# A gated cross-attention block on one core: weight work on other engines, and projections two slots later

## The chip, the cores and the metric

The kernel runs on 1 core of a Trainium2 chip, as one launch. Its engines are TensorE (PE in the profile; PEld is its weight loading), VectorE (DVE), ScalarE (ACT), GpSimd (POOL) and SyncE (SP), which here issues every DMA. The metric is the device time in microseconds; less is better. Each engine works through its own program in order, and the programs meet only at semaphores.

## The reference

One Flamingo-style block on x (4 batches of 512 rows by 512) with a context of the same size, cut to what matters here:

```python
ln  = layernorm(layernorm(x))                              # the second with weights and bias
fp8 = lambda x, s: e4m3(bf16(clip(x / s, -448, 448)))      # back in f32
q, k, v, qx = (fp8(ln, s) * s @ W.T * w_scale for s, W, w_scale in ...)   # 16, 8, 8, 16 heads of 128
kx, vx = split(ctx @ w_kv_x.T)
q, k, qx, kx = head-wise layernorms
core = softmax(q k^T / sqrt(128)) v                        # two query heads share a key head
xout = softmax(qx kx^T / sqrt(128)) vx
x = x + tanh(g0) * (fp8(concat(core, xout), smooth) * ... @ wproj.T)
# feed-forward part, weights in {-1, 0, 1} times a scale
ternary = lambda w: clip(round(w / mean|w|), -1, 1) * mean|w|
h = int8(layernorm(x)) @ ternary(w_gate_up).T;  a, b = split(h)
x = x + tanh(g1) * (int8(silu(a) * b) @ ternary(w_down).T)
```

Products that need f32 accuracy are made of pairs of f16: x = hi + lo, with `hi = f16(x)` and `lo = f16(x - hi)`.

## The kernel before, in words

The attention part is cut into 32 rounds (`it`): 4 batches times 8 head groups. A round has 16 slots, and a slot is one tile of 128 query rows by 512 keys for one query head. All five programs are one long loop over slot numbers n, from `FIRST` = -28 to `PAST` = 532; what an engine does in slot n is picked by the tables at the top of the file. Round `it` has its scores in slots 16 it to 16 it + 15. In a slot TensorE makes the scores (L687, 3 matmuls of 128x512), VectorE takes the row maxima (L971), ScalarE the exponentials (L1319) and, scaled, the f16 hi part (L1330), VectorE the lo part (L981) two slots after the scores, and SyncE turns both by DMA (`pt<-pp`). Scores use PSUM banks 0 to 3 in turn: scores n wait for the lo part of n - 4.

Around that frame the tables put the rest:

- **Projections** of round `it` (`gemm`, L654 and L661) stand in 16 slots before its scores, from slot 16 it - 25 (`GEMM_AT` = 7) to 16 it - 10. A row tile takes four slots: A0, A1 (q and qx, 8 matmuls of 256 columns each), B0 (k and v, 16 of 128), B1 (kx and vx, 12 of 256). Behind A1 and B1 come their statistics (VectorE, L940, L941, L948), the inverse deviations (GpSimd, L1541 to L1554), and the normed tiles (L954, L963 on VectorE; from tile 36 on the B half on ScalarE).
- **Heads** (`head`, L674): when the four row tiles are done, six heads are transposed through PSUM bank 7, read by ScalarE (L1312) and split into hi and lo by GpSimd (L1560, L1566). `HEADS_AT` puts them at slots 9, 12, 14, 16, 18, 22, less 16 (relative to 16 it).
- **Bank 7** also takes the transposes of x for the next batch (`x_turn`, L626, in slots 20, 26, 36 and 52 of a batch, read by ScalarE at L1240 in that slot and the next) and, in rounds 0 to 5, one small product per round that spreads the maximum of the next-but-one group's context weights (`w_whole`, L600, from a tile that GpSimd writes at L1469 one slot earlier). VectorE reads it one slot after (`kv_factor`, L826 to L877). Each use of the bank waits until the one before has been read (`OLDER`).
- **Value products** (`pv`, L699): four per pair of query head and key head, into bank 4, over four slots by `PVS`, counted from slot 9. ScalarE reads the bank (`o_out`, L1338), and the output is quantised by GpSimd (L1572), VectorE (L991, L993, L995) and GpSimd (L1578).
- **Weights of the first batch** are loaded into one of three `raw` buffers, prepared by VectorE, ScalarE and GpSimd over up to eight slots, and used two to three rounds ahead; later batches load the stored result.
- **x of the next batch** is quantised in place (`x_quant`) in 40 slots from slot 62 of a batch, one of five steps per slot: a clip (L910), then four more (L913 to L919), all on VectorE.
- **Late weights**: 129 jobs, one each 8/3 slots (`JOBS_FROM` = 92, `TERN_FROM` = 309). In slots 92 to 302 are 48 sums of absolute values (ScalarE) and 32 *splits* of `wproj`: hi on GpSimd in slot n (L1585), lo on VectorE in n + 1 (L1017), the sum of |lo| on ScalarE in n + 2. In slots 311 to 437 are 48 *ternary* jobs: scale and round on ScalarE in slot n (L1352), then on VectorE in n + 1 the offset off and the upper clip (L1010), and the lower clip (L1011). `fp8` clips elsewhere stay as they are.

After the last slot come the output projection and the feed-forward part, 16 row tiles (L716, L741, L758).

## Time and profile before

| | |
|---|---|
| time, median of 3 runs | 1862.5 us (1860.18 to 1867.15) |
| time of the profiled execution | 1860.7 us |
| its span, first to last instruction | 1858.9 us |
| mean granted TensorE clock | 0.976 of full speed |
| scores of slot 0 begin | 110.0 us |
| row maxima of slot 0 and of slot 511 | 113.9 and 1506.1 us |
| output projection and feed-forward | from about 1527 us |

The span holds three unlike parts: a ramp of 113.9 us, in which weights are prepared and no scores run, 512 slots of attention, and some 330 us of feed-forward work. Within the attention the jobs beside the frame differ from round to round, so a share of busy time over the whole span tells little; the views are read by stage and by round. A group row names the line, engine and operation, output<-inputs, the shape, and then busy us, mean ns of one | idle time of the engine just before them, with what ended it.

### The profile page before, as it was taken

To read this page: it belongs to the slowest core of one execution; us is meant where nothing else is said; L and a number is where in the kernel's file an instruction comes from. 1 tells how busy PE (TensorE), PEld (TensorE's weight loads), DVE (VectorE), ACT (ScalarE), POOL (GpSimd) and SP (SyncE) were. 2 spreads that over 40 slices of the span, in tenths; PEclk is the share of its full clock that TensorE was granted. 3 is DMA by queue.
4 is the path that set the end of the run, shared out by engine and by line. 5 is a ranking of instruction groups with operands and counts; after the bars stand their busy time and mean duration, and the time that the engine had idled before them with its cause. 6 is when DMAs were issued, how large, how long until landed. Compare 5 with 4: busy or idle time off the path is not lost.

```text
span 1858.9 us, 35181 instructions
## 1 busy us (share of the span) xinstructions
PE 1629.7 (88%) x11164; PEld 1007.7 (54%) x11164; DVE 1575.9 (85%) x3451; ACT 1350.9 (73%) x3351; POOL 1095.2 (59%) x1421
## 2 busy tenths in 40 slices
PE   2478899788999998899899888999999879999996
PEld 1355555455656665566566555666666434444442
DVE  7569899999898899988888999999988856777774
ACT  6468998777889987898898788998988842222222
POOL 3677888876776777776777667777767530000000
PEclk9889999999999999999999999999999989999997
DMA  3357899889999998899899998999999966322200
GB/s 101 96 149 168 190 192 211 174 187 193 203 226 202 194 224 180 191 208 249 192 207 200 229 193 195 233 231 222 217 232 181 205 157 214 105 69 80 69 18 17
DMA packets 669597, 325.48 MB, mean 175 GB/s; under 512 B 552288, under 2 KB 595424, under 8 KB 669152
## 3 DMA queue, kind: packets, MB, share of 16 engines
q1 hardware_dynamic: 669408, 323.17, 77.5%
q8 instruction: 93, 1.52, 0.4%
q14 instruction: 96, 0.79, 0.1%
HBM read 140.61 MB, written 48.23 MB: 102 GB/s over the span
## 4 chain that ended last, share of the span: by engine, by line
PE 41%; DVE 26%; POOL 12%; ACT 8%; issue 7%; DMA 4%; SPq 1%; ACTq 0%; DVEq 0%; POOLq 0%
PE psum L699 7%; PE psum L687 6%; PE psum L654 6%; PE psum L741 6%; PE psum L716 6%; DVE pp L981 5%; DVE nmx L971 5%; PE psum L661 3%; DMA pt<-pp 3%; PE psum L758 3%; PE psum L674 2%; POOL wbt L1513 2%; POOL qk L1566 2%; ACT pp L1330 1%; POOL ars L1544 1%
## 5 line engine op out<-in xcount | busy, mean ns | idle before, releaser
L687 PE MATMUL psum<-qk 128*128 128x512 f16 x1536 | 421.9, 384 | 29.0 <-DVE pp L981 22.9
L699 PE MATMUL psum<-pt,vv 128*128 128x512 f16 x1536 | 398.5, 382 | 55.8 <-ACT cy L1338 40.6
L654 PE MATMUL psum<-wbt,xqt 128*128 128x256 f16 (+1 forms) x4096 | 411.3, 251 | 25.1 <-DVE xqt L898 11.1
L654 PEld LDWEIGHTS psum<-wbt,xqt 128*128 128x128 f16 x4096 | 333.6, 100 | 135.5 <-issue 20.4
L1319 ACT ACTIVATE psum<-psum,nmx 128x512 f32<-128x512 f32 x512 | 344.4, 673 | 84.9 <-DVE nmx L971 80.4
L981 DVE SCALAR_TENSOR_TENSOR pp<-psum,prs,pp 128x512 f16<-128x512 f32 x512 | 378.5, 739 | 5.5 <-ACT pp L1330 5.2
L971 DVE TENSOR_REDUCE nmx<-psum 128x1 f32<-128x512 f32 x512 | 344.5, 673 | 36.7 <-PE psum L687 35.2
L1330 ACT ACTIVATE pp<-psum,prs 128x512 f16<-128x512 f32 x512 | 356.7, 697 | 18.5 <-DMA pt<-pp 18.2
L699 PEld LDWEIGHTS psum<-pt,vv 128*128 128x128 f16 x1536 | 147.5, 98 | 252.5 <-issue 70.0
L1566 POOL TENSOR_TENSOR qk<-y,qk 128x512 f16<-128x512 f32 x192 | 233.7, 1217 | 16.0
L687 PEld LDWEIGHTS psum<-qk 128*128 128x128 f16 x1536 | 143.8, 99 | 114.7 <-DVE pp L981 26.0
L661 PE MATMUL psum<-wbt,ctxh 128*128 128x256 f16 x1536 | 190.8, 275 | 0.3 <-POOL wbt L1518 0.3
L661 PEld LDWEIGHTS psum<-wbt,ctxh 128*128 128x128 f16 x1536 | 151.2, 99 | 45.1 <-issue 0.8
L1325 ACT ACTIVATE prs<-psm 128x1 f32<-128x1 f32 x512 | 112.9, 220 | 82.7 <-DVE psm L976 81.0
L1578 POOL TENSOR_TENSOR cy<-cy,cc 128x512 f16<-128x512 bf16 x128 | 153.6, 1201 | 15.7 <-DVE cy L995 13.9
L1646 POOL TENSOR_SCALAR frs<-fmv 128x1 f32<-128x1 f32 x16 | 3.0, 190 | 267.9 <-DVE fmv L1046 267.8
L1312 ACT ACTIVATE y<-psum,hb,hw 128x512 f32<-128x512 f32 x192 | 152.4, 794 | 8.7 <-PE psum L674 8.7
L1541 POOL TENSOR_TENSOR ars<-ast,eps 128x4 f32<-128x4 f32 x128 | 52.3, 409 | 175.1 <-DVE ast L941 174.7
L1437 ACT ACTIVATE sl<-psum,am 128x512 f32<-128x512 f32 x64 | 44.0, 687 | 137.7 <-PE psum L741 137.7
L1560 POOL TENSOR_SCALAR qk<-y 128x512 f16<-128x512 f32 x192 | 121.1, 631 | 38.2 <-ACT y L1312 33.6
L1544 POOL TENSOR_TENSOR ars<-ars,mhalf 128x4 f32<-128x4 f32 x128 | 133.5, 1043 | 10.0
L674 PE MATMUL psum<-idf,xh 128*128 128x128 f32 x768 | 118.9, 278 | 22.7 <-ACT xqt L1240 18.3
(176 smaller groups left out, 2711.1 us busy)
## 6 DMA issues: line engine op xcount, KB each, us to landing
wbt<-ws SPq DMA_DIRECT2D x192, 256.0 KB, 3.8
ws<-wbt SPq DMA_DIRECT2D x64, 256.0 KB, 4.0
catd<-cy SPq DMA_DIRECT2D x64, 256.0 KB, 3.3
...
pt<-pp SPq DMA_TRANSPOSE x512, 3.7
...
```

Source lines behind the costliest of these rows:

```text
L654: ins = e.matmul(bank[:, o0:o0 + c1 - c0], xv[:, v, kt * 512 + tt * 128:kt * 512 + (tt + 1) * 128], wb[i][:, h, kt, c0:c1], start=kt == 0 ...
L661: ins = e.matmul(bank[:, 256:512], ctxh[:, u, kt, ts], wkvb[i][:, w, kt, :], start=kt == 0 and k == 0, stop=kt == 3 and k == 2)
L674: ins = e.transpose(bank[:, tt * 128:(tt + 1) * 128], xh[it % 2][:, tt, j, :], idf[:])
L687: ins = e.matmul(SB(n), qk[i][:, jq, u, ss], qk[i][:, jk, w, :], start=k == 0, stop=k == 2)
L699: ins = e.matmul(OB, v[:, t, u, att, :], src[:, w, t, :], start=t == 0 and k == 0, stop=t == 3 and k == 2)
L971: e.tensor_reduce(nmx[:, n % 8:n % 8 + 1], SB(n), AX, ALU.max, negate=True).then_inc(s["mx"], 1)
L981: e.scalar_tensor_tensor(pp[k][:, 1, :], SB(n), prs[:, n % 8:n % 8 + 1], pp[k][:, 0, :], ALU.mult, ALU.subtract).then_inc(s["lo"], 1)
L1312: e.activation(y32[n % 2][:], psum[:, BANK["T", n], :], ACT.Identity, bias=hb[:, vec:vec + 1], scale=hw[:, vec:vec + 1]).then_inc(s["y32"], 1)
L1319: e.activation(SB(n), SB(n), ACT.Exp, bias=nmx[:, k], accum_out=psm[:, k]).then_inc(s["exp"], 1)
L1330: e.activation(pp[n % 4][:, 0, :], SB(n), ACT.Copy, scale=prs[:, n % 8:n % 8 + 1]).then_inc(s["hi"], 1)
L1566: e.tensor_tensor(qk[it % 2][:, j, 1, :], y32[n % 2][:], qk[it % 2][:, j, 0, :], ALU.subtract).then_inc(s["hd_lo"], 1)
L1578: e.tensor_tensor(y.bitcast(F16), y, tmp, ALU.subtract).then_inc(s["o_q"], 1)
```

## The change

Three things are changed together.

1. **Work of the late weights.** The hi part of a split is made by ScalarE (`job_hi`, slot n) and the lo part by GpSimd (n + 1); VectorE has no part in it. In a ternary job ScalarE scales and rounds as before (n), GpSimd clips both sides in f32 (n + 1, new semaphore `l_tc`), and VectorE takes the offset off in one instruction (n + 2).
2. **Clips of x.** For batches 2 and 3 the eight clips of `x_quant` go to GpSimd (`x_clip`); for batch 1 they stay on VectorE.
3. **The timetable.** Projections, weight loads and stores, the small product of bank 7 and the loads for the last stage stand two slots later relative to the scores; the output steps one slot later; of the heads only the first, from 9 to 10. The loop begins at -26. Value products stand one, two, one, none over four slots, where they stood one, one, two, none. Round 1 may begin its projections when four of its six weight tiles are ready.

```diff
-FIRST, PAST = -28, NSLOT + 20
+FIRST, PAST = -26, NSLOT + 20
-PVS = ((0,), (1,), (2, 3), ())
-GEMM_AT = 7
+PVS = ((0,), (1, 2), (3,), ())
+GEMM_AT = 9
-HEADS_AT = (9, 12, 14, 16, 18, 22)
+HEADS_AT = (10, 12, 14, 16, 18, 22)
...
-POOL_HI = 2
+POOL_HI, POOL_X = 2, 2
...
-                            q.wait_ge("w_dn", it * 6 + (6 if it else 4))
+                            q.wait_ge("w_dn", it * 6 + (6 if it > 1 else 4))
...
@@ VectorE: x_quant
+                if step == 0 and b >= POOL_X:
+                    return
@@ VectorE: job
-                if what in ("sum", "scale"):
+                if JOBS[m][0] != "tern":
                     return
-                    q.wait_ge("l_t1", JV["l_t1", m])
-                    q.done(e.tensor_scalar(ob, f, MAGIC, 1.0, ALU.subtract, ALU.min))
-                    e.tensor_scalar(ob, ob, -1.0, None, ALU.max).then_inc(s["l_t2"], 1)
-                else:
-                    q.wait_ge("l_hi", JV["l_hi", m])
...
-                    e.tensor_tensor(o.bitcast(F16)[:, 0:512], f, wps[:, j, :], ALU.subtract).then_inc(s["l_lo"], 1)
+                q.wait_ge("l_tc", JV["l_tc", m])
...
+                e.tensor_scalar(raw[i][:, 512:768].bitcast(BF16)[:, 0:512], raw[i][:, 0:512], MAGIC, None,
+                                ALU.subtract).then_inc(s["l_t2"], 1)
...
-                if JOB_AT.get(n - 1, -1) >= 0:
-                    job(JOB_AT[n - 1])
+                if JOB_AT.get(n - 2, -1) >= 0:
+                    job(JOB_AT[n - 2])
@@ ScalarE
+            def job_hi(m):
+                j, i = JOBS[m][2], (K0 + m) % 2
+                q.wait_ge(f"raw_ld{i}", JV[f"raw_ld{i}", K0 + m])
+                e.activation(wps[:, j, :], raw[i][:, 0:512], ACT.Copy).then_inc(s["l_hi"], 1)
@@ GpSimd: x_clip and job
+                q.wait_ge("x_w", ((b - 1) * 8 + part) * 4)
+                e.tensor_scalar(src, src, 448.0, -448.0, ALU.min, ALU.max).then_inc(s["x_w"], 1)
...
                 if what == "split":
-                    e.tensor_scalar(wps[:, j, :], raw[i][:, 0:512], 1.0, 1.0, ALU.mult, ALU.mult).then_inc(s["l_hi"], 1)
+                    q.wait_ge("l_hi", JV["l_hi", m])
...
+                    e.tensor_tensor(o.bitcast(F16)[:, 0:512], f, wps[:, j, :], ALU.subtract).then_inc(s["l_lo"], 1)
+                elif what == "tern":
+                    q.wait_ge("l_t1", JV["l_t1", m])
+                    e.tensor_scalar(f, f, MAGIC + 1.0, MAGIC - 1.0, ALU.min, ALU.max).then_inc(s["l_tc"], 1)
...
-                if JOB_AT.get(n, -1) >= 0:
-                    job(JOB_AT[n])
+                if JOB_AT.get(n - 1, -1) >= 0:
+                    job(JOB_AT[n - 1])
```

The lines of the changed kernel are one to ten higher than those of before: L600 becomes L601, L626 L627, L654 L655, L661 L662, L674 L675, L687 L688, L699 L700; on VectorE L948, L954, L971, L976, L981, L991, L993 and L995 become L951, L957, L974, L979, L984, L994, L996 and L998, and L931 becomes L934.

TensorE in round 0, from the small product into bank 7 (`psum<-spread,ones`) to the first head transpose (`psum<-idf,xh`). `psum<-qk` opens a slot, and `psum<-pt,vv` are value products. Before:

```order
L654 MATMUL psum<-wbt,xqt 128x256 x8
L600 MATMUL psum<-spread,ones 128x128
L687 MATMUL psum<-qk 128x512 x3
L654 MATMUL psum<-wbt,xqt 128x256 x8
L687 MATMUL psum<-qk 128x512 x3
L699 MATMUL psum<-pt,vv 128x512 x3
L654 MATMUL psum<-wbt,xqt 128x128 x16
L674 MATMUL psum<-idf,xh 128x128 x4
```

Changed:

```order
L655 MATMUL psum<-wbt,xqt 128x256 x8
L601 MATMUL psum<-spread,ones 128x128
L688 MATMUL psum<-qk 128x512 x3
L700 MATMUL psum<-pt,vv 128x512 x6
L655 MATMUL psum<-wbt,xqt 128x256 x8
L675 MATMUL psum<-idf,xh 128x128 x4
```

Between the two uses of bank 7 stood two openings of a slot, and now stands one; the value products beside them are six matmuls in place of three.

TensorE in slot 26 of the first batch, at the second transpose of x (`psum<-idf,xt`), with the head transpose before it. Before:

```order
L674 MATMUL psum<-idf,xh 128x128 x4
L687 MATMUL psum<-qk 128x512 x3
L699 MATMUL psum<-pt,vv 128x512 x3
L661 MATMUL psum<-wbt,ctxh 128x256 x12
L626 MATMUL psum<-idf,xt 128x128 x4
L687 MATMUL psum<-qk 128x512 x3
```

Changed:

```order
L655 MATMUL psum<-wbt,xqt 128x256 x8
L675 MATMUL psum<-idf,xh 128x128 x4
L627 MATMUL psum<-idf,xt 128x128 x4
L688 MATMUL psum<-qk 128x512 x3
L700 MATMUL psum<-pt,vv 128x512 x3
```

The head transpose stood a slot ahead of the transpose of x, and now directly ahead of it, in the same slot and the same bank.

VectorE in slots 170 to 172 before, from the statistics of a B half, with a split job (`raw<-raw,wps`); `cc<-cy`, `cc<-cc` and `cy<-cy,cc` are the three output steps:

```order
L948 BN_STATS bst<-psum 128x6
L991 TENSOR_SCALAR cc<-cy 128x1024
L1017 TENSOR_TENSOR raw<-raw,wps 128x512
L976 RECIPROCAL psm<-psm 128x1
L971 TENSOR_REDUCE nmx<-psum 128x1
L981 SCALAR_TENSOR_TENSOR pp<-psum,prs,pp 128x512
L931 SCALAR_TENSOR_TENSOR vv<-psum,vv 128x256
L993 TENSOR_SCALAR cc<-cc 128x1024
L976 RECIPROCAL psm<-psm 128x1
L971 TENSOR_REDUCE nmx<-psum 128x1
L981 SCALAR_TENSOR_TENSOR pp<-psum,prs,pp 128x512
L940 BN_STATS ast<-psum 128x6
```

Changed, slots 171 to 173:

```order
L957 TENSOR_TENSOR xh<-psum,ars 128x512
L994 TENSOR_SCALAR cc<-cy 128x1024
L979 RECIPROCAL psm<-psm 128x1
L974 TENSOR_REDUCE nmx<-psum 128x1
L984 SCALAR_TENSOR_TENSOR pp<-psum,prs,pp 128x512
L951 BN_STATS bst<-psum 128x6
L996 TENSOR_SCALAR cc<-cc 128x1024
L979 RECIPROCAL psm<-psm 128x1
L974 TENSOR_REDUCE nmx<-psum 128x1
L984 SCALAR_TENSOR_TENSOR pp<-psum,prs,pp 128x512
L934 SCALAR_TENSOR_TENSOR vv<-psum,vv 128x256
L998 TENSOR_TENSOR cy<-cy,cc 128x1024
```

The split job is gone. The first output step stood behind statistics and now stands behind a normed tile (`xh<-psum,ars`), and the second the other way round: it now follows statistics.

## Rows read from the trace of the kernel before

**Rows 1.** page: busy us (share) xinstructions per engine; the chain by engine.

```profile
PE 1629.7 (88%) x11164; PEld 1007.7 (54%) x11164; DVE 1575.9 (85%) x3451; ACT 1350.9 (73%) x3351; POOL 1095.2 (59%) x1421
...
PE 41%; DVE 26%; POOL 12%; ACT 8%; issue 7%; DMA 4%; SPq 1%; ACTq 0%; DVEq 0%; POOLq 0%
```

**Rows 2.** by stage: us, busy us of PE, PEld, DVE, ACT, POOL, clock, DMA.

```profile
0.00:113.90 113.90, 45.86 (x326) 36.30 (x327) 71.64 (x187) 59.51 (x122) 59.66 (x77) 0.91 0.34 106
113.90:411.50 297.60, 249.90 (x1782) 161.51 (x1779) 273.23 (x609) 253.48 (x649) 244.48 (x303) 0.97 0.84 181
411.50:1163.20 751.70, 686.16 (x5060) 453.91 (x5060) 685.23 (x1480) 642.97 (x1681) 537.67 (x700) 0.99 0.95 206
1163.20:1440.70 277.50, 274.81 (x2074) 185.29 (x2073) 255.57 (x572) 248.03 (x632) 200.50 (x268) 1.00 1.02 219
```

**Rows 3.** one or two rounds of sixteen slots, same columns.

```profile
671.70:767.30 95.60, 83.90 (x609) 54.91 (x606) 93.07 (x195) 74.85 (x201) 67.84 (x84) 0.98 0.94 201
811.70:850.40 38.70, 38.70 (x295) 26.11 (x293) 34.91 (x78) 36.12 (x100) 30.27 (x42) 1.00 1.06 219
1023.80:1118.40 94.60, 82.88 (x603) 52.87 (x601) 94.09 (x217) 76.77 (x189) 64.12 (x78) 1.00 0.97 213
1202.40:1242.10 39.70, 39.23 (x298) 26.38 (x296) 38.59 (x86) 36.44 (x93) 28.94 (x39) 1.00 1.03 234
```

**Rows 4.** VectorE groups, 411.5 to 1163.2 us; busy us, mean ns, idle before.

```profile
L1017 DVE TENSOR_TENSOR raw<-raw,wps 128x512 f16<-128x512 f32 x32 | 34.6, 1083 | 9.4 <-POOL wps L1585 9.3
L993 DVE TENSOR_SCALAR cc<-cc 128x1024 bf16<-128x1024 bf16 x34 | 29.8, 876 | 0.0
L910 DVE TENSOR_SCALAR xqt<-xqt 128x1024 bf16<-128x1024 bf16 x17 | 9.2, 543 | 0.0
L1010 DVE TENSOR_SCALAR raw<-raw 128x512 bf16<-128x512 f32 x21 | 12.0, 570 | 0.0
L1011 DVE TENSOR_SCALAR raw<-raw 128x512 bf16<-128x512 bf16 x21 | 7.0, 334 | 0.7
```

**Rows 5.** waits, 411.5 to 1163.2 us: us in total, times, longest us.

```profile
POOL ars L1541 <- DVE ast L941: 101.1, 59, 3.6
PE psum L699 <- ACT cy L1338: 26.6, 20, 3.9
PE psum L674 <- ACT xqt L1240: 10.5, 7, 2.0
PE psum L606 <- POOL spread L1476: 6.2, 2, 3.5
```

**Rows 6.** time order, one split job: VectorE, then GpSimd (start us, us).

```profile
911.99 1.63 DVE L1017 TENSOR_TENSOR raw<-raw,wps 128x512 f16<-128x512 f32 x1 [1.38 <-POOL wps L1585]
...
911.92 1.15 POOL L1578 TENSOR_TENSOR cy<-cy,cc 128x512 f16<-128x512 bf16 x1
```

**Rows 7.** time order, round 2, bank 7: TensorE, then VectorE.

```profile
243.86 0.81 PE L687 MATMUL psum<-qk 128*128 128x512 f16 x3
...
239.87 0.27 DVE L826 TENSOR_REDUCE wmx<-psum 128x1 f32<-128x128 f32 x1
240.81 0.23 DVE L877 TENSOR_SCALAR wmean<-wmean,wfa 128x4 f32<-128x4 f32 x1
245.76 0.16 DVE L976 RECIPROCAL psm<-psm 128x1 f32<-128x1 f32 x1
```

**Rows 8.** time order, the ramp: TensorE.

```profile
91.29 1.03 PE L654 MATMUL psum<-wbt,xqt 128*128 128x256 f16 x8 [4.35 <-POOL wbt L1518]
110.04 1.46 PE L687 MATMUL psum<-qk 128*128 128x512 f16 x3 [4.21 <-POOL qk L1566]
```

**Rows 9.** groups of the whole run: GpSimd, then ScalarE.

```profile
L1566 POOL TENSOR_TENSOR qk<-y,qk 128x512 f16<-128x512 f32 x192 | 233.7, 1217 | 16.0
L1560 POOL TENSOR_SCALAR qk<-y 128x512 f16<-128x512 f32 x192 | 121.1, 631 | 38.2 <-ACT y L1312 33.6
...
L1277 ACT ACTIVATE wbt<-raw 128x512 f16<-128x512 f32 x4 | 2.4, 624 | 0.1
```

More of the change, by code:

```diff
@@ L43 @@
 KV_PREP = {"part": 2, "mid": 6, "hi": 7, "lo": 8}
-STORE_W = 8
-POOL_HI = 2
+STORE_W = 10
+POOL_HI, POOL_X = 2, 2
 ACT_NORM = 9 * 4
-WG_AT, CAT_AT, X2_AT = (444, 488), (472, 496), 506
+WG_AT, CAT_AT, X2_AT = (444, 490), (474, 498), 507
 RAMP = -4
-OUT_AT = {"clip": 17, "field": 18, "step": 19, "add": 20, "sub": (21, 23), "store": 26}
+OUT_AT = {"clip": 18, "field": 19, "step": 20, "add": 21, "sub": (22, 24), "store": 27}
 JOBS_FROM, TERN_FROM = 92, 309
@@ L66 @@
     "mid": (90, 92, 94, 96),
-    "parts": (102, 102, 102, 102),
+    "parts": (104, 104, 104, 104),
 }
@@ L186, in job_tables @@
             up("l_t1", m)
+            up("l_tc", m)
             up("l_t2", m)
@@ L512, in sp_program @@
                     turn(n - 3)
-                nw, j = divmod(n + 8 + 2 * SLOTS, SLOTS)
+                nw, j = divmod(n + 6 + 2 * SLOTS, SLOTS)
                 if j < 8 and NG <= nw < NIT:
@@ L998, in job @@
             def job(m):
-                what, src, j, _ = JOBS[m]
+                if JOBS[m][0] != "tern":
+                    return
                 i = (K0 + m) % 2
-                f, o = raw[i][:, 0:512], raw[i][:, 512:768]
-                if what in ("sum", "scale"):
-                    return
                 stored, summed = JB[m]
-                if what == "tern":
-                    ob = o.bitcast(BF16)[:, 0:512]
-                    q.wait_ge("l_t1", JV["l_t1", m])
-                    q.wait_ge(f"l_st{i}", JV[f"l_st{i}", stored])
-                    q.wait_ge("l_ab", JV["l_ab", summed])
-                    q.done(e.tensor_scalar(ob, f, MAGIC, 1.0, ALU.subtract, ALU.min))
-                    e.tensor_scalar(ob, ob, -1.0, None, ALU.max).then_inc(s["l_t2"], 1)
-                else:
-                    q.wait_ge("l_hi", JV["l_hi", m])
-                    if stored is not None:
-                        q.wait_ge(f"l_st{i}", JV[f"l_st{i}", stored])
-                        q.wait_ge("l_ab", JV["l_ab", summed])
-                    e.tensor_tensor(o.bitcast(F16)[:, 0:512], f, wps[:, j, :], ALU.subtract).then_inc(s["l_lo"], 1)
+                q.wait_ge("l_tc", JV["l_tc", m])
+                q.wait_ge(f"l_st{i}", JV[f"l_st{i}", stored])
+                q.wait_ge("l_ab", JV["l_ab", summed])
+                e.tensor_scalar(raw[i][:, 512:768].bitcast(BF16)[:, 0:512], raw[i][:, 0:512], MAGIC, None,
+                                ALU.subtract).then_inc(s["l_t2"], 1)
             def weight_sums():
@@ L1420, in act_program @@
                     ctx_hi(b, kt)
+                if JOB_AT.get(n, -1) >= 0 and JOBS[JOB_AT[n]][0] == "split":
+                    job_hi(JOB_AT[n])
                 for at in (n, n - 2):
@@ L1533, in x_rstd, with x_clip @@
                 e.tensor_tensor(r[3], r[0], r[1], ALU.mult).then_inc(s["x_rs"], 1)
+            def x_clip(b, k):
+                part = k // 5
+                v, half_ = divmod(part, 2)
+                src = xq[b % 2][:, v, half_ * 1024:(half_ + 1) * 1024]
+                q.wait_ge("xy", xy_value(b, 3, v))
+                q.wait_ge("x_w", ((b - 1) * 8 + part) * 4)
+                e.tensor_scalar(src, src, 448.0, -448.0, ALU.min, ALU.max).then_inc(s["x_w"], 1)
             def rstd_a(it, tt):
@@ L1582, in job @@
                 i = (K0 + m) % 2
+                f, o = raw[i][:, 0:512], raw[i][:, 512:768]
                 if what == "split":
-                    q.wait_ge(f"raw_ld{i}", JV[f"raw_ld{i}", K0 + m])
-                    e.tensor_scalar(wps[:, j, :], raw[i][:, 0:512], 1.0, 1.0, ALU.mult, ALU.mult).then_inc(s["l_hi"], 1)
+                    stored, summed = JB[m]
+                    q.wait_ge("l_hi", JV["l_hi", m])
+                    if stored is not None:
+                        q.wait_ge(f"l_st{i}", JV[f"l_st{i}", stored])
+                        q.wait_ge("l_ab", JV["l_ab", summed])
+                    e.tensor_tensor(o.bitcast(F16)[:, 0:512], f, wps[:, j, :], ALU.subtract).then_inc(s["l_lo"], 1)
+                elif what == "tern":
+                    q.wait_ge("l_t1", JV["l_t1", m])
+                    e.tensor_scalar(f, f, MAGIC + 1.0, MAGIC - 1.0, ALU.min, ALU.max).then_inc(s["l_tc"], 1)
             q.wait_ge("pre_v", 1)
@@ L1634, in pool_program @@
                     x_rstd(b)
+                for b, k in x_steps(n, "quant"):
+                    if k % 5 == 0 and b >= POOL_X:
+                        x_clip(b, k)
                 for b, _ in x_steps(n, "cxs"):
```

10 lines of the change are left out of this document (5 added, 5 removed).

## The prediction, made before the changed kernel was run

> **What bounds the kernel now.** First the page's totals and chain [rows 1]: TensorE leads with 88% busy and VectorE follows with 85%, and the chain is shared, 41% and 26%. No single engine bounds the span, so it has to be read by stage. The stages [rows 2] show where each has slack. In the ramp nobody is full (TensorE 46 of 114 us). From 113.9 to 411.5, rounds 0 to 5, VectorE is busy 273, ScalarE 253, TensorE 250 and GpSimd 244 of 298 us: a crowd. From 411.5 to 1163.2, rounds 6 to 22, TensorE has 686 and VectorE 685 of 752. From 1163.2 to 1440.7 TensorE has 274.8 of 277.5 and nothing else matters. Single rounds [rows 3] show the pattern inside the long stage: a round costs 38.7 to 39.7 us where TensorE is full, and 47 to 48 where VectorE is (93.1 of 95.6 us in one pair of rounds, 94.1 of 94.6 in another). Those pairs carry the quantising of x besides split or ternary jobs.
>
> So VectorE's work is worth time in rounds 6 to 22 and none in rounds 23 to 29. The whole margin: 17 rounds at 39.7 would be 674.9 us, and 751.7 are spent, 76.8 too many. Of these, TensorE's own waits put 10.5 on ScalarE's reading of the transposed x and 6.2 on a tile of GpSimd [rows 5], which the change does not touch. 60.1 us are open to it.
>
> **Weight work off VectorE, 411.5 to 1163.2.** All 32 splits are there: 34.6 us busy and 9.4 idle ahead of them, 44.0 [rows 4]. Of the 17 clips of x at 543 ns, 16 go, 8.7. Of a ternary job's two instructions at 570 and 334 ns one is left. It has the first's shape, so I keep 570 and take away the second: 21 times, 7.0 busy and 0.7 idle. In sum 60.4 us of VectorE. What of it the span gets lies between two ends. The low end counts only the four rounds that VectorE fills [rows 3]: by the tables they hold 6 splits, 12 clips that go and 12 ternary jobs, 6.5 + 6.5 + 4.0 = 17 us. The high end is 60, all the open margin. In rounds not filled on average a split still hurts: one waited 1.38 us for GpSimd's half and then took 1.63, since GpSimd had begun another instruction 0.07 us before [rows 6], a hole of 3 us that the four score banks cannot wholly cover; the 26.6 us for which value products wait on ScalarE's output copy [rows 5] come behind such holes. Both ends have their rounds, and I take the middle, 38. In the 27 ternary jobs after 1163.2 the saving is nothing: TensorE is full. Late next is TensorE itself.
>
> **What the other engines get in that stretch.** GpSimd: 32 times a subtraction at 1217 ns in place of a copy at 631 (both by the rows of the same shapes [rows 9]), 19 us, 16 clips of 1024 bf16 numbers, each between one and two of the 631 ns for 512 f32 ones, 10 to 20, and 21 ternary clips at 631, 13. That makes 42 to 52 on top of 538 of 752 [rows 2], still under 80%. ScalarE: 32 copies at 624 ns [rows 9], 20 us on 643. They are covered by the slack of both; if cover fails, inverse deviations come late and VectorE's normed tiles with them. I charge 4 us, with 0 and 10 as ends.
>
> On GpSimd and VectorE the rows show that they block each other: the split above, and the second output step, whose mean is 876 ns for 1024 bf16 numbers while the clip of the same size has 543 [rows 4]. The Trainium skill (SBUF, "Who interferes with whom") says that VectorE's two-port and two-input forms and GpSimd instructions hold one port pair exclusively, and whichever starts first makes the other wait to its end; its page Perfetto Trace Analysis ("Optimizing Scalar/DVE Operations") warns that shifting work between just these two might not help. This trace agrees with the first. By the second the charge of 4 would be nearer the 10; the numbers here would stay within my range.
>
> **Output steps.** They move by one slot, and the first now follows a normed tile and the second follows statistics (third piece of order). Statistics are what GpSimd waits for, so the second step should meet it idle, and the first, behind a GpSimd job just released, should not. 34 steps at 876 could fall to 543: 11 us less. The first could rise by the same. I take nothing, with 11 either way here, and 20 for the attention as a whole (64 pairs).
>
> **The ramp and the end.** Round 1's projections waited 4.35 us for the last two weight tiles [rows 8]; that condition is relaxed and the wait goes. Scores of slot 0 begin two slots sooner relative to projections, yet there they already waited 4.21 us for a head from GpSimd [rows 8], which stays on the path. So 4.35 and about half a slot more: 6 us gained, with 0 and 9 as ends. At the end two slots get projections that had none, at most 2 times the difference, which I put at 1 us each: 2 lost. Net 4 gained.
>
> **Bank 7: the wait that the change adds.** In rounds 0 to 5 the small product moves from slot 7 to 9 of a round and the first head from 9 to 10, so the one-slot gap for VectorE's reading is gone (first piece of order). TensorE in slot 10 must now wait for the reading, which stands last in VectorE's slot 10. From the trace of round 2 [rows 7]: TensorE ended that slot at 243.86 and VectorE at 245.76, and the reading takes from 239.87 to 240.81 plus 0.23, 1.17 us, so it would end at 246.9 and TensorE waits 3.1. Behind the waiting transpose stand the scores of slot 11, and for these VectorE and ScalarE wait. VectorE resumes only after four transposes and three score matmuls; the latter take 0.81 us [rows 7], and with half a microsecond for the former, an estimate, that is 1.3. TensorE's 3.1 is partly lead that it had; the 1.3 is lost by all. Six times, 8 us; ends 0 and 18 (6 times 3.1).
>
> Similarly, in slot 26 of batches 0, 1 and 2, the transpose of x now stands directly behind a head in the same slot (second piece). TensorE waits there for ScalarE to read the head. The reading is a ScalarE instruction on 128x512 numbers, not under the 624 ns of the copy [rows 9]; the most is the 4 us of one and a half slots. Three times, that is 2 to 12, and I take 5.
>
> **Sum**, against the profiled execution's 1860.7 (span 1858.9): -38 -4 +8 +5 +4 +0 = -25, so 1835.7. The median of the runs shown stands 1.8 above the profiled one, so 1837.5.
>
> **Rivals.**
> - *VectorE was busy but not the bound* outside the filled rounds: only 17 us come. For it: in rounds at 40 to 45 us VectorE has holes too, and ScalarE's 643 of 752 sits in the loop. Against it: the 3 us holes at splits. 1860.7 - 17 - 4 + 17 = 1856.7, as a median 1858.5: no change that can be told.
> - *The phase of output steps is a stroke of luck*: the second step falls to 543 and the first stays; GpSimd is idle when VectorE gets there. For it: GpSimd waits 101 us for statistics in this stretch alone [rows 5]. Against it: the gain is worth nothing where TensorE is full. The 64 second steps give 64 times 333 ns, 21 us, and 1837.5 less most of that is 1817.5. That is also what the port rule gives if issue order favours VectorE.
> - *Bank 7 costs its full price* and turns the change slower. Every head waits behind the bank's last reader, at the place where TensorE is a slot or more ahead; if the lead is not rebuilt, 18 and 12 are lost instead of 8 and 5, and the two later slots leave no margin elsewhere either, so that GpSimd's charge is 10 and the ramp yields nothing but loses the 2 of the end. With the relief at 17: 1860.7 - 17 + 2 + 18 + 12 + 10 = 1885.7; with the relief at 38, 1864.7. Half way, 1877 as a median. It decides from the point at which these waits exceed the relief.
> - *The change does not do what it says*, VectorE staying as busy since the remaining ternary instruction is blocked by the new GpSimd clips: at most 21 times 1.15 us [rows 6], 24 of the 60 us; the relief of 38 shrinks in that proportion by 15, and the median is 1852.5, at the edge of the first rival's case.
>
> **How the numbers follow.** Forecast 0.60, the first rival with the last 0.15, the luck of phase 0.15, slower 0.10. What a measurement of this kernel can tell from no change is 0.5%, 9.3 us: below 1853.2 is faster, above 1871.8 slower. The forecast's own range is 1824 to 1854 (relief 25 to 55, other terms against it). Faster: nearly all of the forecast and the luck, 0.74; same: 0.17; slower: 0.09. The range for 8 in 10 goes from 1813 to 1864.
>
> **What would show it.** Right: rounds 12, 13, 20 and 21 at 42 to 44 us in place of 47 to 48; VectorE's busy time in rounds 6 to 22 down by 50 or more; rounds 23 to 28 still 39 to 40; scores of slot 0 some 6 us sooner relative to the start; head transposes that wait for `wfa` or `xt` readings on VectorE and ScalarE, about 3 us each, in slots 10 and 26. Wrong: filled rounds that stay above 46 us with VectorE no longer busy in them (then a loop of latencies bounds), head waits in every round, or VectorE instructions of over 1 us in many more places than before.

## The result: slower by 3.1%, and the profile after

| | before | changed |
|---|---|---|
| median, runs taken together | 1862.75 us (4 runs) | 1920.88 us (4 runs, 1916.57 to 1924.39) |
| ratio, 95% interval | | 1.031 (1.0293 to 1.0327) |
| time and span of the profiled execution | 1860.7, 1858.9 | 1916.6, 1914.8 |

The forecast was 1837.5, the range ended at 1864, and the slower rival stood at 1877: the result lies outside all of them. The page of the changed kernel, totals and chain, beside [rows 1]:

```profile
PE 1645.9 (86%) x11147; PEld 1010.5 (53%) x11164; DVE 1528.6 (80%) x3355; ACT 1367.3 (71%) x3383; POOL 1140.0 (60%) x1485
...
PE 35%; POOL 24%; DVE 19%; ACT 10%; issue 8%; DMA 3%; SPq 1%; POOLq 0%; ACTq 0%; DVEq 0%
```

VectorE did lose work, 1575.9 to 1528.6, and GpSimd gained 45. But GpSimd's share of the chain doubled, 12% to 24%, at 60% busy. An engine can take the chain without being full, if what others need stands late in its queue.

By stage (ramp, rounds 1 to 5, 6 to 22, 23 to 26, then the pairs 12, 13 and 20, 21; columns as in [rows 2, 3]):

```profile
0.00:110.60 110.60, 43.82 (x310) 34.78 (x310) 68.04 (x180) 57.94 (x118) 55.49 (x72) 0.77 0.31 96
...
159.60:441.90 282.30, 221.01 (x1512) 139.71 (x1510) 238.80 (x514) 216.60 (x551) 208.43 (x251) 0.94 0.75 165
441.90:1199.70 757.80, 695.01 (x5075) 456.28 (x5076) 646.54 (x1412) 658.88 (x1715) 567.29 (x738) 0.98 0.94 205
1199.70:1375.60 175.90, 161.38 (x1188) 104.59 (x1187) 141.83 (x322) 147.67 (x368) 128.95 (x177) 1.00 0.97 210
695.00:792.70 97.70, 85.47 (x599) 54.43 (x596) 85.49 (x186) 77.19 (x204) 72.22 (x89) 0.95 0.90 191
1048.50:1150.30 101.80, 85.10 (x588) 53.40 (x589) 87.82 (x198) 76.81 (x187) 76.79 (x96) 0.95 0.86 187
```

| us | before | changed |
|---|---|---|
| ramp, to the row maxima of slot 0 | 113.9 | 110.6 |
| round 0 | 49.6 | 49.1 |
| rounds 1 to 5 | 248.0 | 282.2 |
| rounds 6 to 18 | 569.5 | 560.1 |
| rounds 19 to 27 | 381.2 | 413.5 |
| of these, rounds 23 to 26 | 159.5 | 175.9 |
| pair 12, 13; pair 20, 21 | 95.6; 94.6 | 97.7; 101.8 |

The loss has two places: 34 us in rounds 1 to 5, before the jobs of the late weights begin (slot 92), and 32 in rounds 19 to 27, where the ternary jobs are. Between them 9 us were gained. In the two filled pairs VectorE is no longer full (85.5 of 97.7), yet they are longer: the prediction's own sign for "a loop of latencies bounds". Rounds 23 to 26 took 44.0 each in place of 39.1 to 40.9. TensorE, which I held to be all that mattered there, is busy 161 of 176.

The same stretch as [rows 4, 5], rounds 6 to 22, groups and then waits:

```profile
L1588 POOL TENSOR_TENSOR cy<-cy,cc 128x512 f16<-128x512 bf16 x68 | 79.0, 1162 | 0.0
...
L1601 POOL TENSOR_TENSOR raw<-raw,wps 128x512 f16<-128x512 f32 x32 | 38.6, 1207 | 3.0 <-ACT wps L1338 2.9
...
L998 DVE TENSOR_TENSOR cy<-cy,cc 128x1024 bf16<-128x1024 bf16 x34 | 27.6, 811 | 0.0
...
L994 DVE TENSOR_SCALAR cc<-cy 128x1024 uint16<-128x1024 uint16 x34 | 24.7, 725 | 9.2 <-POOL cy L1582 9.2
...
L1543 POOL TENSOR_SCALAR xqt<-xqt 128x1024 bf16<-128x1024 bf16 x16 | 17.4, 1088 | 1.2
L1604 POOL TENSOR_SCALAR raw<-raw 128x512 f32<-128x512 f32 x21 | 15.2, 723 | 1.8
L996 DVE TENSOR_SCALAR cc<-cc 128x1024 bf16<-128x1024 bf16 x34 | 14.6, 429 | 0.0
...
L1010 DVE TENSOR_SCALAR raw<-raw 128x512 bf16<-128x512 f32 x21 | 8.9, 424 | 17.1 <-POOL raw L1604 17.1
```

```profile
POOL ars L1551 <- DVE ast L944: 136.5, 59, 8.0
...
DVE raw L1010 <- POOL raw L1604: 17.1, 17, 2.5
...
PE psum L700 <- ACT cy L1332: 15.7, 20, 1.6
...
DVE xtmp L916 <- POOL xqt L1543: 14.5, 10, 3.1
...
POOL brs L1562 <- DVE bst L951: 8.0, 6, 2.3
```

The second output step (L996) fell from 876 to 429 ns, now that it follows statistics. The first (L994) and the third (L998) rose to 725 and 811. Before, in the same stage, they and GpSimd's wait for the statistics of the B halves stood so:

```profile
L995 DVE TENSOR_TENSOR cy<-cy,cc 128x1024 bf16<-128x1024 bf16 x34 | 22.8, 669 | 0.0
...
L991 DVE TENSOR_SCALAR cc<-cy 128x1024 uint16<-128x1024 uint16 x34 | 14.0, 412 | 2.1 <-POOL cy L1572 2.1
...
POOL brs L1552 <- DVE bst L948: 64.2, 46, 2.8
```

VectorE's busy time in the stage fell by 38.7 (685.2 to 646.5) rather than the expected 50 or more. GpSimd waits longer for the statistics of the A halves (101.1 to 136.5) and hardly any more for those of the B halves (64.2 to 8.0), so in sum less. Two waits appear that did not exist before: VectorE for the ternary clip (17.1) and for the clip of x (14.5, in the rounds in which x is quantised), both of which GpSimd now makes. In rounds 23 to 26, where x is not quantised, the first is large:

```profile
POOL ars L1551 <- DVE ast L944: 35.9, 16, 3.5
DVE raw L1010 <- POOL raw L1604: 30.1, 25, 2.6
...
PE psum L688 <- DVE pp L984: 8.6, 8, 1.7
```

25 waits in 64 slots, with a job every 8/3 slots: about one in every job. One of them, first VectorE, then GpSimd, in order of time (start us, us, and the idle time before in brackets):

```profile
1304.41 0.41 DVE L944 BATCH_NORM_STATS2 ast<-psum 128x6 f32<-128x256 f32 x1
...
1306.23 0.69 DVE L957 TENSOR_TENSOR xh<-psum,ars 128x512 f32<-128x512 f32 x1
1309.47 0.43 DVE L1010 TENSOR_SCALAR raw<-raw 128x512 bf16<-128x512 f32 x1 [2.55 <-POOL raw L1604]
```

```profile
1304.91 0.20 POOL L1551 TENSOR_TENSOR ars<-ast,eps 128x4 f32<-128x4 f32 x1 [3.48 <-DVE ast L944]
1305.19 1.01 POOL L1554 TENSOR_TENSOR ars<-ars,mhalf 128x4 f32<-128x4 f32 x1
1306.16 1.16 POOL L1588 TENSOR_TENSOR cy<-cy,cc 128x512 f16<-128x512 bf16 x1
1307.42 0.27 POOL L1485 TENSOR_SCALAR kfac<-cmx,wmx 128x1 f32<-128x1 f32 x1
...
1308.47 0.27 POOL L1488 TENSOR_SCALAR kfac<-aco,kfac 128x2 f32<-128x2 f32 x1
1308.82 0.61 POOL L1604 TENSOR_SCALAR raw<-raw 128x512 f32<-128x512 f32 x1
```

GpSimd gets the statistics at 1304.9, and then does in one slot the deviation, an output subtraction (1.16), four factor instructions and last the clip (0.61), which ends at 1309.43. VectorE has been idle since 1306.92, and its next row maximum, for which ScalarE and then TensorE wait, stands behind that clip.

Of bank 7 and the weight tiles, whole run:

```profile
PE psum L655 <- POOL wbt L1514: 20.7, 7, 5.0
...
PE psum L675 <- DVE wfa L830: 9.7, 6, 1.6
```

The new head wait that I priced highest came to at most 1.6 us at a time. Waits for weight tiles went from 9.6 us in 3 to 20.7 in 7; the one of 4.3 us in the ramp that the relaxed condition takes away is not counted in the 9.6.

### The profile page after: what moved, and what is told of

Read it like the earlier page. It is cut to its first block, busy times and chain, and to the rows that moved or that the text cites. A ratio compares the mean times of both kernels' runs of the same rounds, so it can differ in the third digit from the quotient of the medians.

```text
span 1914.8 us, 35172 instructions
## 1 busy us (share of the span) xinstructions
PE 1645.9 (86%) x11147; PEld 1010.5 (53%) x11164; DVE 1528.6 (80%) x3355; ACT 1367.3 (71%) x3383; POOL 1140.0 (60%) x1485
## 4 chain that ended last, share of the span: by engine, by line
PE 35%; POOL 24%; DVE 19%; ACT 10%; issue 8%; DMA 3%; SPq 1%; POOLq 0%; ACTq 0%; DVEq 0%
PE psum L742 6%; PE psum L700 6%; PE psum L717 5%; PE psum L655 5%; PE psum L688 5%; DVE nmx L974 4%; DVE pp L984 4%; POOL ars L1554 4%; POOL cy L1588 3%; PE psum L759 3%; POOL qk L1576 3%; DMA pt<-pp 2%; POOL qk L1570 2%; PE psum L662 2%; POOL cy L1582 2%
## 5 line engine op out<-in xcount | busy, mean ns | idle before, releaser
L688 PE MATMUL psum<-qk 128*128 128x512 f16 x1536 | 426.6, 387 | 39.8 <-DVE pp L984 39.1
L700 PE MATMUL psum<-pt,vv 128*128 128x512 f16 x1536 | 405.8, 388 | 50.8 <-ACT cy L1332 38.4
L655 PE MATMUL psum<-wbt,xqt 128*128 128x256 f16 (+1 forms) x4096 | 412.2, 250 | 35.3 <-POOL wbt L1514 20.7
L1313 ACT ACTIVATE psum<-psum,nmx 128x512 f32<-128x512 f32 x512 | 344.7, 673 | 94.6 <-DVE nmx L974 92.2
L655 PEld LDWEIGHTS psum<-wbt,xqt 128*128 128x128 f16 x4096 | 332.3, 100 | 149.6 <-issue 30.6
L984 DVE SCALAR_TENSOR_TENSOR pp<-psum,prs,pp 128x512 f16<-128x512 f32 x512 | 379.0, 740 | 5.9 <-ACT pp L1324 5.8
L974 DVE TENSOR_REDUCE nmx<-psum 128x1 f32<-128x512 f32 x512 | 345.1, 674 | 45.4 <-PE psum L688 44.6
L700 PEld LDWEIGHTS psum<-pt,vv 128*128 128x128 f16 x1536 | 148.6, 99 | 255.9 <-issue 55.5
L1576 POOL TENSOR_TENSOR qk<-y,qk 128x512 f16<-128x512 f32 x192 | 227.9, 1187 | 16.0
L688 PEld LDWEIGHTS psum<-qk 128*128 128x128 f16 x1536 | 143.5, 100 | 128.1 <-DVE pp L984 35.2
L662 PE MATMUL psum<-wbt,ctxh 128*128 128x256 f16 x1536 | 194.0, 277 | 0.3 <-POOL wbt L1519 0.3
L1551 POOL TENSOR_TENSOR ars<-ast,eps 128x4 f32<-128x4 f32 x128 | 31.6, 247 | 270.6 <-DVE ast L944 270.4
L662 PEld LDWEIGHTS psum<-wbt,ctxh 128*128 128x128 f16 x1536 | 152.6, 100 | 46.8 <-issue 1.4
L1588 POOL TENSOR_TENSOR cy<-cy,cc 128x512 f16<-128x512 bf16 x128 | 148.2, 1159 | 17.1 <-DVE cy L998 17.1
L1570 POOL TENSOR_SCALAR qk<-y 128x512 f16<-128x512 f32 x192 | 140.4, 731 | 27.4 <-ACT y L1306 18.8
L675 PE MATMUL psum<-idf,xh 128*128 128x128 f32 x768 | 118.5, 278 | 34.1 <-ACT xqt L1234 19.8
```

The costliest lines, as they stand in the source:

```text
L655: ins = e.matmul(bank[:, o0:o0 + c1 - c0], xv[:, v, kt * 512 + tt * 128:kt * 512 + (tt + 1) * 128], wb[i][:, h, kt, c0:c1], start=kt == 0 ...
L662: ins = e.matmul(bank[:, 256:512], ctxh[:, u, kt, ts], wkvb[i][:, w, kt, :], start=kt == 0 and k == 0, stop=kt == 3 and k == 2)
L688: ins = e.matmul(SB(n), qk[i][:, jq, u, ss], qk[i][:, jk, w, :], start=k == 0, stop=k == 2)
L700: ins = e.matmul(OB, v[:, t, u, att, :], src[:, w, t, :], start=t == 0 and k == 0, stop=t == 3 and k == 2)
L974: e.tensor_reduce(nmx[:, n % 8:n % 8 + 1], SB(n), AX, ALU.max, negate=True).then_inc(s["mx"], 1)
L984: e.scalar_tensor_tensor(pp[k][:, 1, :], SB(n), prs[:, n % 8:n % 8 + 1], pp[k][:, 0, :], ALU.mult, ALU.subtract).then_inc(s["lo"], 1)
```

## The experiments

A ratio is to the kernel before, on the same chip. Stage times are of one profiled execution of each. The theory that stands at the end: the moved work gives a little, the timetable costs, and most of the cost is what now stands ahead of others in GpSimd's queue. Its main rival: the first heads behind bank 7, as in the slower rival of the prediction.

**The halves alone.** `time_only` has the new tables with all work where it was; `work_only` the moved work and clips in the old tables.

```diff
 time_only: tables at the top, and the round 1 wait, of the changed kernel
 work_only: the changed kernel with all tables, and that wait, as before
-GEMM_AT = 9
+GEMM_AT = 7
...
```

> The timetable of the change alone (projections two slots later, heads, output steps, value products one, two, one, the relaxed wait of round 1); the weight work and the clips of x stay as before. Theory (two separate losses: rounds 1 to 5 lost 34 us by the timetable, through the shortened distances in bank 7 and the weight preparation, and rounds 19 to 27 lost 32 us by the ternary jobs' detour over GpSimd): rounds 1 to 5 take 275 to 285 us as in the changed kernel (before: 248), rounds 23 to 26 stay at 39 to 40 us each, in sum 1890 us. Rival (the timetable itself puts VectorE's statistics, GpSimd's deviations and VectorE's normed tiles into a tight loop, and the ternary jobs only show it): rounds 23 to 26 are at 42 to 44 us here too, in sum 1910 or more.

> The weight work of the change alone (splits on ScalarE and GpSimd, ternary clips and the clips of x on GpSimd) in the timetable of before. Theory: rounds 1 to 5 as before (248 us), rounds 6 to 18 some 20 us less than before (576), rounds 23 to 26 at 44 us each as in the changed kernel, because VectorE waits for GpSimd's ternary clip in any timetable; in sum 1865 to 1880 us. Rival (timetable and ternary jobs only hurt together): rounds 23 to 26 at 39 to 40 us, in sum 1830 to 1840 us.

Measured: `time_only` 1900.66, 1.0208 (1.0175 to 1.0242), about 39 us slower; `work_only` 1851.1, 0.9954 (0.9935 to 0.9973), 9 us faster, rounds 6 to 18 in 558.4 for 569.5. Together they would be 30 slower; the changed kernel is 58. So some 28 us are an interaction, give or take 8 by the intervals. In `time_only` rounds 1 to 5 take 286.3 and rounds 23 to 26 40.3 each, as its theory said, though the time is 11 us above it. In `work_only` rounds 23 to 26 take 40.0 each: that theory, with 44 in any timetable, falls, and the rival was right on the rounds but 11 us too hopeful on the time.

Groups of `work_only` in rounds 6 to 22:

```profile
L996 DVE TENSOR_SCALAR cc<-cc 128x1024 bf16<-128x1024 bf16 x34 | 29.6, 870 | 0.0
...
L1604 POOL TENSOR_SCALAR raw<-raw 128x512 f32<-128x512 f32 x21 | 13.9, 664 | 1.8
L1010 DVE TENSOR_SCALAR raw<-raw 128x512 bf16<-128x512 f32 x21 | 10.6, 505 | 2.5 <-POOL raw L1604 2.5
```

With the queue of the old tables the ternary step hardly waits for GpSimd (2.5 us in all), and L996 still takes 870 ns. The wait for the clip of x is 3.9 us in 5.

**The ternary jobs.** `after_tern_back` is the changed kernel with its ternary jobs as before; `after_tern_first` only puts GpSimd's ternary clip first in its slot.

```diff
 after_tern_first, GpSimd, at the head of the slot
+                if JOB_AT.get(n - 1, -1) >= 0 and JOBS[JOB_AT[n - 1]][0] == "tern":
+                    job(JOB_AT[n - 1])
...
-                if JOB_AT.get(n - 1, -1) >= 0:
+                if JOB_AT.get(n - 1, -1) >= 0 and JOBS[JOB_AT[n - 1]][0] != "tern":
```

> The changed kernel with the ternary jobs as before: both clips on VectorE, one slot after ScalarE's part, nothing on GpSimd. Theory: VectorE's 50 us of waits for GpSimd's clip go, rounds 19 to 27 fall from 414 us to 380 (before: 381), rounds 1 to 5 stay at 282, in sum 1886 us. Rival (the timetable makes the loop tight): rounds 19 to 27 stay over 400 us, in sum 1905 or more.

> The changed kernel with GpSimd's ternary clip first in its slot, ahead of the inverse deviations and the output steps; nothing else moves. Theory (in the new timetable GpSimd's output steps stand in the slots of the statistics, and the clip behind them comes after VectorE is due to read it one slot later: VectorE waits 50 us in 44 of 48 jobs): the waits fall below 10 us, rounds 23 to 26 take 40 to 41 us each in place of 44.0, rounds 19 to 27 390 us in place of 414, in sum 1895 us. Rival (the extra GpSimd time or its hold on the port is what costs, wherever it stands): rounds 23 to 26 stay at 43 us or more, in sum 1912 or more.

Measured: `after_tern_back` 1893.56, 1.0187 (1.0154 to 1.0221), and `after_tern_first` 1891.27, 1.0155 (1.013 to 1.018). The same clip by the same engine, only earlier in its slot, gives back 29 us; having no such clip gives back 23. Rounds 23 to 26 of `after_tern_first` take 157.6, or 39.4 each: before had 159.5, and its rival expected 43 or more each. Its waits in these rounds:

```profile
POOL raw L1604 <- ACT raw L1351: 14.8, 8, 2.8
...
DVE raw L1010 <- POOL raw L1604: 1.8, 4, 0.5
```

VectorE's wait fell from 30.1 to 1.8, and GpSimd now waits for ScalarE instead, which costs the span nothing there. GpSimd has the same work in both, so this part of the loss is the clip's place in the queue, neither GpSimd's load nor blocking. It is about as large as the interaction.

**Value products.** `after_old_pvs` has `PVS` of before in the changed kernel.

```diff
-PVS = ((0,), (1, 2), (3,), ())
+PVS = ((0,), (1,), (2, 3), ())
```

> The changed kernel with the value products as before, one, one, two, none. Theory (their place is of no account where VectorE or its partners bound): within 5 us of the changed kernel, 1916 to 1926 us. Rival (two value products ahead of the second half of the q projections make its statistics late, and that is what tightens the loop through GpSimd): rounds 23 to 26 fall from 44.0 to 41 or less, VectorE's wait for the projections (30 us in the changed kernel) goes, in sum 1905 or less.

Measured: 1910.91, 1.0269 (1.0238 to 1.03). Their new order costs about 8 us, with 7 either way by the intervals, rather than gaining. Rounds 23 to 26 stay at 43.9 each, so the rival of this run falls, and its theory, that their place is of no account, is 5 us off.

**The weights of rounds 1 to 5, and the head behind bank 7.** Both edits in `time_only`: `time_prep_early` prepares weights at the old slots; `time_head_11` gives four of the six new bank 7 waits a slot of distance.

```diff
 time_prep_early
-TILE_LOAD = (-6, -2, -1, 1, -11, -10)
-RAMP_LOAD = (-27, -26, -25, -20, -18, -17)
+TILE_LOAD = (-8, -4, -3, -1, -13, -12)
+RAMP_LOAD = (-27, -26, -25, -22, -20, -19)
 time_head_11
+        if o == 0:
+            if it in (1, 3, 4, 5):
+                j -= 1
```

> The timetable of the change alone (weight work as before), but with the weight preparation of rounds 2 to 7 at its old slots, relative to the scores (loads at -8, -4, -3, -1, -13, -12 and in the ramp at -22, -20, -19). The small product in bank 7 is back at slot 7, three slots ahead of the head at 10, and the weights are ready two slots earlier for the first projection at slot 9. Theory (the 38 us that the timetable loses in rounds 1 to 5 come from the chain weights, small product, its reading, head, which holds TensorE and VectorE alternately in slots 9 and 10): rounds 1 to 5 take 248 to 256 us in place of 286, in sum 1865 us. Rival (the new phase of projections, statistics and output steps against the weight work on GpSimd makes these rounds slow): they stay above 275 us, in sum 1890 or more.

> The timetable of the change alone, with the first head of rounds 1, 3, 4 and 5 at slot 11 in place of 10, so that VectorE has a slot to read the small product again; the head of round 2 stays at 10. Theory (the wait of the head for this reading is the larger part of the chain in slots 9 and 10): rounds 2, 3 and 4 take 4 to 6 us less each than with the timetable alone (54.2, 54.6, 61.3), round 1 stays at 58. Rival (the wait of the first projection for its weights in slot 9 is what costs, and the head's wait only follows): rounds 2 to 4 fall by less than 2 us each.

Measured: `time_prep_early` 1888.99, 1.015 (1.012 to 1.018), rounds 1 to 5 in 267.7 for 286.3. `time_head_11` 1901.77, 1.0213 (1.017 to 1.0256), not to be told from 1.0208, and intervals of that width would hide some 10 us. In its profiled execution rounds 1 to 5 are 5.0 us shorter than in `time_only` (rounds 2 to 4 by 2.7, 0.6 and 0.3), the ramp 2.7 longer and the part behind round 27 1.7 longer. The bank 7 rival falls as the main cause: 5 us of the 38 that the timetable adds in rounds 1 to 5. Waits of `time_prep_early`, whole run:

```profile
PE psum L600 <- POOL spread L1469: 37.5, 8, 13.4
...
PE psum L654 <- POOL wbt L1513: 3.4, 1, 3.4
```

The wait for weight tiles is down from 23.8 us in 7 to 3.4 in 1. The one for the small product's input rose (21.7 in `time_only`), and still rounds 1 to 5 are 19 us shorter: it was the tiles for the most part. This edit also takes away the head waits behind bank 7 (9.7 us in `time_only`), which are worth at most the 5 us of `time_head_11`. The theory of this run, 248 to 256 us, was only half right. And the whole kernel gained only 11 us by ratio: the ramp and round 0 became 5.4 us longer (111.9 and 52.0 for 108.5 and 50.0).

**The output steps.** `after_out_before` takes back `OUT_AT` in the changed kernel, `time_out_before` in the timetable alone, and `before_out_after` makes that one move alone on the kernel before.

```diff
-OUT_AT = {"clip": 18, "field": 19, "step": 20, "add": 21, "sub": (22, 24), "store": 27}
+OUT_AT = {"clip": 17, "field": 18, "step": 19, "add": 20, "sub": (21, 23), "store": 26}
```

> The changed kernel with the output steps (clip, three on VectorE, two subtractions, store) at the slots of before, one earlier; projections, heads and value products stay changed. GpSimd's clip and subtractions then stand in odd slots, the statistics' deviations in even ones. Theory (the same as for the clip first in its slot): the ternary waits of VectorE fall from 50 to under 20 us, rounds 23 to 26 take 40 to 41.5 us each, in sum 1893 to 1900 us. Rival (the phase of the output steps is of no account): rounds 23 to 26 stay at 44 us, in sum 1915 to 1925.

> The kernel before with one table changed: the output steps one slot later, as in the change; nothing else. Theory (the output steps of GpSimd must not share a slot with the statistics: these stand in even slots before and after, since projections moved by two, while clip and subtractions went from odd to even slots): most of the timetable's loss appears here alone, rounds 1 to 5 at 262 to 275 us in place of 248, in sum 1880 to 1900 us. Rival (the one-slot move hurts only together with the later projections): within 8 us of before.

> The timetable of the change alone, without its move of the output steps. Theory (output steps carry most of the timetable's 40 us, the later weight preparation the rest in rounds 1 to 5): 1860 to 1870 us, rounds 1 to 5 at 265 to 272 us, rounds 6 to 27 within 6 us of before. Rival (the output steps' move hurts only with the weight work on GpSimd): 1890 us or more.

| by ratio x 1862 | steps as before | one slot later | the move costs |
|---|---|---|---|
| kernel before | 0 | +22 (1884.98; 1.0119, 1.0085 to 1.0153) | 22 |
| timetable alone | +7 (1868.82; 1.0037, 1.002 to 1.0054) | +39 | 32 |
| changed kernel | +12 (1872.18; 1.0065, 1.0039 to 1.0091) | +58 | 46 |

One slot of the output steps is the largest single part of the loss, and costs something without the rest of the change. It is spread out: of the 32 us in the timetable alone, 17 lie in rounds 1 to 5 (286.3 for 268.9). The expectations were right on the time of `time_out_before` and `before_out_after`, and `after_out_before` came out over 20 us better than its theory. Why it costs: statistics stand in even slots of VectorE, before as after, and GpSimd's deviations behind them. Its output clip (1.04 us) and subtractions (1.16 each) stood in the odd slots between, and now share a slot with the deviations. The same ternary job as above in `after_out_before`, GpSimd, then VectorE:

```profile
1269.08 1.01 POOL L1554 TENSOR_TENSOR ars<-ars,mhalf 128x4 f32<-128x4 f32 x1
...
1271.59 0.61 POOL L1604 TENSOR_SCALAR raw<-raw 128x512 f32<-128x512 f32 x1
...
1274.33 1.15 POOL L1588 TENSOR_TENSOR cy<-cy,cc 128x512 f16<-128x512 bf16 x1
```

```profile
1272.23 0.43 DVE L1010 TENSOR_SCALAR raw<-raw 128x512 bf16<-128x512 f32 x1 [1.25 <-POOL raw L1604]
```

The subtraction stands behind the clip now instead of ahead of it, and VectorE's wait is 1.25 us in place of 2.55: shorter by just about that 1.16.

In `before_out_after` there is no ternary clip on GpSimd, and the output clip itself is what comes late. Its groups for rounds 6 to 22, and one place in time order, GpSimd, then VectorE:

```profile
L991 DVE TENSOR_SCALAR cc<-cy 128x1024 uint16<-128x1024 uint16 x34 | 14.9, 437 | 39.2 <-POOL cy L1572 38.8
L993 DVE TENSOR_SCALAR cc<-cc 128x1024 bf16<-128x1024 bf16 x34 | 13.9, 408 | 0.0
```

```profile
1027.51 0.19 POOL L1552 TENSOR_TENSOR brs<-bst,eps 128x2 f32<-128x2 f32 x1 [1.95 <-DVE bst L948]
...
1028.47 0.62 POOL L1560 TENSOR_SCALAR qk<-y 128x512 f16<-128x512 f32 x1
1029.17 1.16 POOL L1566 TENSOR_TENSOR qk<-y,qk 128x512 f16<-128x512 f32 x1
1030.41 1.04 POOL L1572 TENSOR_SCALAR cy<-cy 128x1024 bf16<-128x1024 bf16 x1
```

```profile
1028.91 0.41 DVE L931 SCALAR_TENSOR_TENSOR vv<-psum,vv 128x256 f16<-128x256 f32 x1
1031.48 0.43 DVE L991 TENSOR_SCALAR cc<-cy 128x1024 uint16<-128x1024 uint16 x1 [2.15 <-POOL cy L1572]
```

The second step fell from 876 to 408 ns, 15.9 us less VectorE work in this stage, just what my "luck of phase" rival hoped for. But ahead of the first step VectorE now waits 38.8 us for GpSimd's clip, where it waited 2.1 before: the clip stands behind a deviation (for which GpSimd waited) and a head's hi and lo parts (0.62 and 1.16). All three steps together are 53.9 us busy here (14.9, 13.9 and 25.1) against 66.6 before, and the kernel is still 22 us slower: the blocked second step had been the cheap side of that choice. In the timetable alone it is the split job that waits, VectorE for GpSimd's hi part: 17.2 us in rounds 6 to 22 of `time_only`, 6.2 in those of `time_out_before`. In rounds 1 to 5 there are no such jobs, and by which wait their 17 us come is not shown. No run moved GpSimd's output steps without VectorE's, so what each side costs by itself is not shown.

**Mended, and the relaxed wait.** `mended` is the changed kernel with the three repairs (output steps, ternary clip first, weights early). `work_relaxed` is `work_only` with round 1's relaxed condition.

```diff
 mended: after_out_before with the edits of after_tern_first and time_prep_early
 work_relaxed
-                            q.wait_ge("w_dn", it * 6 + (6 if it else 4))
+                            q.wait_ge("w_dn", it * 6 + (6 if it > 1 else 4))
```

> The changed kernel with the three mends together: output steps at the slots of before, ternary clip first in GpSimd's slot, weight preparation of rounds 2 to 7 at the slots of before. Theory (separate causes, each taken away): rounds 1 to 5 at 250 to 258 us, rounds 6 to 18 at 555, rounds 19 to 27 at 380 to 385, in sum 1845 to 1858 us. Rival (the two-slot move of the projections has a price of its own in rounds 1 to 5): these stay at 265 us or more, in sum 1865 or more.

> The weight work of the change in the timetable of before, with one more line of the change: round 1 may begin its projections when four of its six weight tiles are ready. Theory (the weight work is a small gain in itself, 9 us, and the relaxed wait gives back the 4.4 us for which TensorE waited in the ramp): 1845 to 1849 us, the ramp at 107 to 110 us in place of 112. Rival (the ramp's end is set by the heads from GpSimd): ramp within 1 us of 112, 1851 us.

Measured: `mended` 1856.04, 0.9969 (0.9954 to 0.9984); `work_relaxed` 1852.82, 0.9944 (0.9929 to 0.996). The three repairs give 252.2 us for rounds 1 to 5, 552.8 for 6 to 18 and 384.3 for 19 to 27, all about as expected. They take back about 64 us of the changed kernel, but the new tables still bring nothing over the old ones: `work_only` and `work_relaxed` are the fastest, ahead of both kernels, and their intervals overlap, so the relaxed wait adds nothing that can be told. Its ramp is 113.1 us for 112.2, where the theory had 107 to 110.

`mended` has 50.2 and 53.0 us in rounds 13 and 21, where `work_only` has 45.8 and 46.7. A part of this is the third job given to GpSimd, the clip of x, which stands late in its slot too. In round 13 of `mended`, GpSimd, then VectorE:

```profile
740.81 1.04 POOL L1543 TENSOR_SCALAR xqt<-xqt 128x1024 bf16<-128x1024 bf16 x1
```

```profile
741.88 0.43 DVE L916 TENSOR_SCALAR xtmp<-xqt 128x1024 uint16<-128x1024 uint16 x1 [3.12 <-POOL xqt L1543]
```

Such waits are 3.5 us in round 13 and 3.0 in round 21, and 10.4 in the whole run. No run gave the clips of x back or put them first, so their price, and the rest of the difference, stays open.

## Why the prediction was wrong

The step that failed is the term "Output steps: I take nothing, with 11 either way here, and 20 for the attention". Made alone on the kernel before, the move costs 22 us, and in the changed kernel 46. I priced how the two engines' instructions lengthen each other, and in the changed kernel that sum came out at nothing, as I had written: over the three steps, 66.6 us busy before (412, 876, 669 ns x34) and 66.9 after (725, 429, 811), though the third step had no part in my sum. What I left out is the queue: a clip or subtraction of 1.0 to 1.2 us that stands in a slot with the deviations delays whatever follows it on GpSimd, and whoever waits for that. The statement "statistics are what GpSimd waits for, so the second step should meet it idle" read the 101 us of [rows 5] as slack. My reading now is that they were margin in which GpSimd caught up; no run was made for that alone. Blocking by itself does not explain the loss. By the Trainium skill (SBUF, "Who interferes with whom") a VectorE instruction in a two-port mode and a GpSimd instruction take a shared port pair in turn, and the later one waits for the whole of the other. The trace agrees, in that the second step takes 876 or 408 ns by its slot alone; but where the steps were least lengthened, in `before_out_after`, the kernel was slower, and the wait of 2.55 us for the ternary clip began 1.9 us before that clip did. The Trainium skill also warns (Perfetto Trace Analysis, "Optimizing Scalar/DVE Operations") that moving work between just these two engines might not help. Here it gained 9 us in the old tables.

Point by point:
- *Relief of VectorE, -38.* `work_only` shows -9 for all moved work, GpSimd's and ScalarE's extra included, where my two terms gave -34. My low end of 17, less the 4 charged, is nearer than the middle I took. The filled pairs gained little (before 95.6 and 94.6; `work_only` 91.4 and 93.6), so VectorE was busy there but not alone the bound. The first rival was right on this term. The waits of value products on ScalarE, which I counted for a large relief, did fall (26.6 to 15.7 in the changed kernel, 19.8 in `work_only`), and bought nothing that can be seen.
- *Ternary jobs after 1163.2: "the saving is nothing".* No saving, but a cost: 23 us by `after_tern_back`, 29 by `after_tern_first`. TensorE at 274.8 of 277.5 [rows 2] says that its cover was complete, not that it could bear a new wait of 2.5 us in every job. The fourth rival named this pair of instructions, but as blocking, with 24 us of relief lost at most; the wait is for the clip's place in the queue.
- *Bank 7, +8.* The waits are real (9.7 us in 6), the longest 1.6, and giving four of them a slot more took 5.0 us off rounds 1 to 5 and nothing that can be told off the time. *Slot 26, +5*: TensorE's waits ahead of the transposes of x for the reading of a head grew from 1.4 us in 2 to 2.6 in 3. Both were right in kind and smaller than I had them.
- *The ramp, -6.* 3.3 us came. Missing altogether is what followed: weights two slots later leave rounds 1 to 5 waiting for tiles, up to 19 us there by `time_prep_early`, 11 in the whole kernel. I counted the relaxed wait of round 1 as the whole effect of the weight tables, and asked of no later round whether its tiles were in time.
- *Rounds 23 to 28 "still 39 to 40"*: 44.0 for four of them, 39.9 and 41.6 for the last two.
- The slower rival had the sign and the wrong mechanism. It was put at 1877, and even with all its terms at their worst it reached only 1885.7, of the profiled execution. The bounds were too near because the only added waits that they priced were those of bank 7; the others were sums of instruction times.

Shares of the 58 us, by undoing one thing at a time (they overlap, so they don't add up): output steps 46, ternary clip's place 29, late weights 11 in the timetable alone, value products 8, against -9 for the work itself. The clips of x have no share here, since no run took them back alone.
